# Decoder layer on one core: block-by-block weight products, bias products in column strips, and a first operand copied earlier

## What is computed

```python
q = (x @ wq.T + bq) @ vq.T + cq          # k and v alike
scores = einsum('cbqh,cbkh->cbqk', q, k) / 4      # 32 heads of 16, 4 sequences
o = softmax(scores) @ v;  x = layernorm(x + (o @ wo.T + bo))
conv of kernel size 2 over x (512 -> 2048 channels) + ctx + bias, then LSTM-like gates
x = layernorm(x + [h, c])
x = layernorm(x + dequantised(x) @ (ternary - 1).T + b)
```

## Time and profile before

| | us |
|---|---|
| median of three runs | 2178.78 (2175.0 to 2186.28) |
| profiled execution | 2176.87 |
| its span | 2174.9 |
| TensorE busy | 2090.4 |
| VectorE busy | 1662.9 |
| ScalarE busy | 1313.5 |
| GpSimd busy | 491.3 |

### The profile page before, as it was taken

One profiled execution on the slowest core, in us unless ns is written; L12 is line 12 of the kernel. 1 busy time (PEld: TensorE's weight loads), 2 busy tenths in 40 slices (PEclk: granted clock), 3 DMA queues, 4 the chain that ended last, 5 costly groups with the idle time before them and its releaser, 6 DMA issues. The chain is left out here.

```text
span 2174.9 us, 39902 instructions
## 1 busy us (share of the span) xinstructions
PE 2090.4 (96%) x11304; PEld 1178.6 (54%) x11304; DVE 1662.9 (76%) x1725; ACT 1313.5 (60%) x2429; POOL 491.3 (23%) x972
## 2 busy tenths in 40 slices
PE   8999999999999999999999999999999899988996
PEld 3788775444444444444444444444444477766773
DVE  2333355889899999999989899999998377886786
ACT  0121112778788888888888888888887543443344
POOL 0000000111221221212122122212212372555244
PEclk9999999999999999999999999999999999999997
DMA  4355834564665565564665656656657568744672
GB/s 160 97 155 144 198 107 103 90 131 91 133 134 101 128 140 99 126 135 100 136 128 100 138 114 114 137 94 133 134 101 211 165 229 305 288 174 155 228 265 78
DMA packets 205965, 315.24 MB, mean 145 GB/s; under 512 B 105168, under 2 KB 105168, under 8 KB 193616
## 3 DMA queue, kind: packets, MB, share of 16 engines
q1 hardware_dynamic: 205904, 314.47, 57.5%
HBM read 211.06 MB, written 101.19 MB: 144 GB/s over the span
## 5 line engine op out<-in xcount | busy, mean ns | idle before, releaser
L191 DVE TENSOR_REDUCE neg_max<-psum 128x1 f32<-128x1024 f32 x1024 | 1206.9, 1219 | 137.5 <-PE psum L184 137.4
L558 ACT ACTIVATE probs<-psum 128x512 f32<-128x512 f32 x2048 | 1065.4, 607 | 279.5 <-PE psum L485 277.4
L485 PE MATMUL psum<-q_op,k_op 50*128 50x512 f32 x2048 | 751.7, 450 | 10.6 <-DVE v_op L575 5.2
L485 PEld LDWEIGHTS psum<-q_op,k_op 50*128 50x128 f32 x2048 | 353.8, 192 | 586.7 <-ACT probs L558 567.3
L184 PE MATMUL psum<-k_op,q_op 48*128 48x512 f32 x2048 | 625.2, 482 | 0.0
L494 PE MATMUL psum<-probs,v_op 128*32 128x512 f32 x4096 | 547.2, 606 | 5.8 <-ACT probs L558 2.9
L184 PEld LDWEIGHTS psum<-k_op,q_op 48*128 48x128 f32 x2048 | 390.0, 315 | 23.9 <-issue 8.8
L202 POOL CAST neg_max_parts<-neg_max 128x8 fp32r<-128x8 f32 x128 | 25.2, 197 | 1130.1 <-DVE neg_max L191 1130.1
L149 PE MATMUL psum<-x_wino,conv_w 128*128 128x512 f32 x1152 | 275.2, 395 | 1.1 <-DMA conv_w<-conv_w_parts_dram 1.1
L149 PEld LDWEIGHTS psum<-x_wino,conv_w 128*128 128x128 f32 x1152 | 214.6, 188 | 47.0 <-issue 1.5
L494 PEld LDWEIGHTS psum<-probs,v_op 128*32 128x32 f32 x4096 | 82.5, 108 | 137.0 <-ACT probs L558 78.9
(11 more groups left out here) (99 smaller groups left out, 1692.8 us busy)
## 6 DMA issues: line engine op xcount, KB each, us to landing
q_op<-qk_parts_dram SPq DMA_DIRECT2D x384, 128.0 KB, 4.1
conv_w<-conv_w_parts_dram SPq DMA_DIRECT2D x32, 1536.0 KB, 6.7
qk_parts_dram<-qk_parts SPq DMA_DIRECT2D x128, 256.0 KB, 3.2
k_op<-qk_parts_dram SPq DMA_DIRECT2D x384, 64.0 KB, 4.0
conv_w_parts_dram<-conv_w_parts SPq DMA_DIRECT2D x16, 1536.0 KB, 6.1
attended_dram<-out SPq DMA_DIRECT2D x64, 256.0 KB, 2.2
attended_parts_dram<-o_parts SPq DMA_DIRECT2D x128, 128.0 KB, 2.2
gates<-in_ctx_dram SPq DMA_DIRECT2D x32, 512.0 KB, 7.7
```

What stands on the lines that cost most here:

```text
L191: nc.vector.tensor_reduce(ops["max"][b][:, t:t + 1], mem["pair"][t % 2][:], AX_X, ALU.max, negate=True).then_inc(ops["maxed"], 1)
L485: nc.tensor.matmul(score_bank(i, n, j, last), kop[i][r, j // 2, n // 2 * P:(n // 2 + 1) * P], qop[i][r, j // 2, j % 2 * HALF:(j % 2 + 1) * ...
L558: nc.scalar.activation(probs[n % DEEP][:, j, :], score_bank(k, n, j, last), ACT.Exp, scale=SCALE).then_inc(exp_done, 1)
```

## The change

In `combine`: each piece pair of the query weights has its own semaphore. TensorE goes through the pieces in the outer loop and the four groups in the inner one, so four banks are summed at once. The bias loads are issued after the query weights, ahead of the key weights. The query and key biases come from eight matmuls of 512 moving columns. Their stationary operand is a bias column repeated 32 times, and each of the four (two weights, two halves of the sum) has its own strip of 32 rows of bank 6. VectorE copies bank 6 to `rows`, and four small matmuls with a selecting operand `pick` bring each 128 entries back into columns (and sum the halves). Bias work and the two x splits now stand between the groups. In `project` and `attend`: `v_op` and its fills move to the start of `project` (behind those of `k_op0` and `k_op1`). The first copy of values moves to `project`, as GpSimd's first act there, waiting for the sixteenth value group. TensorE's wait for `ones` at the start of `attend` becomes 4. SP's waits become 5 and 6, which are the same two fills, of `k_op2` and `k_op3`.

```diff
@@ combine, SP @@
+                        done = first_in[c] if s == 0 else w_in[s]
+                        chunk = slice(c * P, (c + 1) * P)
+                        sp.dma_start(wn[s][:, c, :], w_nat[s][chunk, :]).then_inc(done, DMA)
+                        sp.dma_start(vt[s][:, c, :], v_t[s][chunk, :]).then_inc(done, DMA)
+                    if s == 0:
+                        for i in range(2):
+                            sp.dma_start(bc[i][:], b_cols[i]).then_inc(bias_in, DMA)
+                            sp.dma_start(vbc[i][:], vb_cols[i]).then_inc(bias_in, DMA)
+                        sp.dma_start(bvc[:], bv_cols).then_inc(bias_in, DMA)
+                        sp.dma_start(vvb[:], vvb_row.broadcast_to([P, F])).then_inc(bias_in, DMA)
@@ combine, TensorE @@
+                for kc in range(KC):
+                    pe.wait_ge(first_in[kc], 2 * DMA)
                     for mt in range(KC):
-                        if g >= BANKS:
-                            pe.wait_ge(comb_out, g - BANKS + 1)
-                        for kc in range(KC):
...
+                        mm = term(0, mt, kc)
+                        if kc == KC - 1:
+                            mm.then_inc(comb, 1)
+                pe.wait_ge(w_in[1], 2 * KC * DMA)
+                for mt in range(KC):
+                    group(1, mt)
+
+                pe.wait_ge(wide_made, 3)
+                for half in range(2):
+                    for j in range(4):
+                        kc = j % 2 * 2 + half
+                        mm = nc.tensor.matmul(bank[6][VW * j:VW * j + VW, :], b_wide[j // 2][:, kc, :], vt[j // 2][:, kc, :],
+                                              start=(half == 0), stop=(half == 1))
+                mm.then_inc(rows_full, 1)
+                pe.wait_ge(w_in[2], 2 * KC * DMA)
                 for kc in range(KC):
                     mm = nc.tensor.matmul(bank[7], bv_wide[:, kc, :], vt[2][:, kc, :],
                                           start=(kc == 0), stop=(kc == KC - 1))
+                mm.then_inc(v_bias_made, 1)
+                for mt in range(2):
+                    group(2, mt)
+
+                pe.wait_ge(rows_made, 5)
+                for mt in range(KC):
+                    mm = nc.tensor.matmul(bank[6][:, 2 * mt:2 * mt + 2], rows[:, mt * P:(mt + 1) * P], pick[:],
+                                          start=True, stop=True)
                 mm.then_inc(bias_made, 1)
+                for mt in range(2, KC):
+                    group(2, mt)
@@ combine, VectorE, in the loop over the twelve groups @@
+                    if g == 5:
+                        split_x_block(nc, dve, x, 0, 0, DMA)
+                    if g == 2 * KC - 1:
+                        dve.wait_ge(rows_full, 1)
+                        nc.vector.tensor_copy(rows[:], bank[6]).then_inc(rows_made, 1)
+                    if g == 2 * KC:
+                        dve.wait_ge(v_bias_made, 1)
+                        nc.vector.tensor_tensor(v_bias[:], bank[7], vvb[:], ALU.add).then_inc(bias_out, 1)
+                    if g == GROUPS - 3:
+                        split_x_block(nc, dve, x, 1, 1, DMA)
+                        dve.wait_ge(bias_made, 1)
...
@@ project @@
+                for i in range(2):
+                    nc.vector.memset(ops["v"][i][:, :, DH:VW], 1.0).then_inc(ops["ones"], 1)
...
+                pool.wait_ge(v_out, KC + BLK // 2 * KC)
+                copy_values(nc, pool, ops, v_sb, 0, 0)
@@ attend @@
-                sp.wait_ge(ones, 3)
+                sp.wait_ge(ones, 5)
...
-                        sp.wait_ge(ones, 4)
+                        sp.wait_ge(ones, 6)
...
-                pe.wait_ge(ones, 6)
+                pe.wait_ge(ones, 4)
...
-                for i in range(2):
-                    nc.vector.memset(vop[i][:, :, DH:VW], 1.0).then_inc(ones, 1)
...
-                values(0, 0)
```

More of the change, by code:

```diff
@@ L51, in combine @@
         bvc = sb("bv_cols", [P, KC], F32)
+        b_wide = [sb(f"b_wide{s}", [P, KC, VW], F32) for s in range(2)]
         bv_wide = sb("bv_wide", [P, KC, P], F32)
         vvb = sb("vvb", [P, F], F32)
-        w_in = [sem(f"w_in{s}") for s in range(3)]
+        rows = sb("bias_rows", [P, F], F32)
+        pick = sb("pick_rows", [P, 2], F32)
+        first_in = [sem(f"w_in0{c}") for c in range(KC)]
+        w_in = [None, sem("w_in1"), sem("w_in2")]
         bias_in = sem("bias_in")
-        bv_made = sem("bv_made")
+        wide_made = sem("wide_made")
         comb = sem("comb")
@@ L59, in combine @@
         comb_out = sem("comb_out")
+        rows_full = sem("bias_rows_full")
+        rows_made = sem("bias_rows_made")
         bias_made = sem("bias_made")
+        v_bias_made = sem("v_bias_made")
         bias_out = sem("bias_out")
@@ L92, in _ @@
-                pe.wait_ge(bias_in, 6 * DMA)
-                for s in range(2):
-                    for mt in range(KC):
-                        for kc in range(KC):
-                            mm = nc.tensor.matmul(bank[6][:, s * KC + mt:s * KC + mt + 1],
-                                                  vt[s][:, kc, mt * P:(mt + 1) * P], bc[s][:, kc:kc + 1],
-                                                  start=(kc == 0), stop=(kc == KC - 1))
-                mm.then_inc(bias_made, 1)
@@ L100, in _, with term, group @@
-                pe.wait_ge(bv_made, 1)
+                def term(s, mt, kc):
+                    return nc.tensor.matmul(bank[(s * KC + mt) % BANKS], wn[s][:, kc, mt * P:(mt + 1) * P],
+                                            vt[s][:, kc, :], start=(kc == 0), stop=(kc == KC - 1))
+                def group(s, mt):
+                    if s * KC + mt >= BANKS:
+                        pe.wait_ge(comb_out, s * KC + mt - BANKS + 1)
+                    for kc in range(KC):
+                        mm = term(s, mt, kc)
+                    mm.then_inc(comb, 1)
@@ L117, in _ @@
                     nc.vector.tensor_tensor(lo, bank[g % BANKS], hi.bitcast(F32), ALU.subtract).then_inc(comb_out, 1)
[L118 to L124 removed]
+                    if g == 5:
[9 more added lines that the diff above has]
+                        dve.wait_ge(bias_made, 1)
+                        by_s = bank[6][:, 0:2 * KC].rearrange("p (m s) -> p s m", s=2)
+                        for s in range(2):
+                            nc.vector.tensor_tensor(qk_bias[:, s, :], by_s[:, s, :], vbc[s][:], ALU.add).then_inc(bias_out, 1)
 def load_x_block(sp, x, x_t, i, first):
@@ L359, in attend @@
         qop, kop = ops["q"], ops["k"]
-        vop = [sb(f"v_op{i}", [P, 2 * QT, VW], F32) for i in range(2)]
+        vop = ops["v"]
         probs = [sb(f"probs{i}", [P, TILES, HALF], F32) for i in range(DEEP)]
@@ L1444, in build @@
                 "max_in": [[sem(f"max_in{i}{b}") for b in range(2)] for i in range(4)],
+                "v": [sb(f"v_op{i}", [P, 2 * QT, VW], F32) for i in range(2)],
+                "v_ready": sem("v_ready"),
                 "ones": sem("ones"),
```

53 lines of the change are left out of this document (20 added, 33 removed).

## The result

| | us |
|---|---|
| median of five runs of the changed kernel | 2163.71 (2161.57 to 2167.43) |
| median of five runs of the kernel before, beside them | 2178.50 (2175.0 to 2186.28) |
| ratio | 0.9932, 95% interval 0.9908 to 0.9955 |
| profiled execution of the changed kernel, and its span | 2167.43, 2165.4 |

The change takes 14.8 us off. 19.9 were forecast. The profiled execution is the slowest of its five, 3.7 above their median, so its parts are read one by one and not summed against the median.

The account below looks back on a forecast made before the run. TensorE, busy 96% of the span, was taken as the bound. Gains of 17.2 (before the projection), 1.6 (clock) and 1.1 (attention) sum to 19.9 us, forecasting 2158 us, range 2150 to 2168.

Parts of the forecast that it names:

- The forecast's own case: Whole kernel: the summed gain of 19.9 us is kept, giving 2158 us; chance 0.66.
- rival B: Small costs (strips not side by side, clock falls at projection and slot 1) take part of the gain: 2166 us; chance 0.17.
- rival D: Attention: SP late, the wait for maxima recurs at each slot; slower, 2191 us if in 20 slots; chance 0.03.
- rival A: Attention: transfers after the barrier go faster and all gain is kept, 6.1 us more, 2152 us; chance 0.08.
- The start, 6.4 us: Start of combine: first matmuls need only two weight loads, so TensorE starts at 4.2 us, not 10.65.
- Rival C: Start of combine: first weight chunks land with the rest, so 6.4 us go: 2164 us; chance 0.06.
- 48 matmuls in 43.2 us: Combine: the 48 weight matmuls keep the earlier kernel's duration of 43.2 us.
- Bias loads at no cost: Combine: bias loads ahead of the key weights cost nothing; key weights land by about 17.5 us, covered by 2.5 us.
- Bias products 6.7: Combine: strips 2.0, value bias 3.6, selecting products 1.1, together 6.7 us in place of 14.5, gaining 7.8.
- Combine, 17.2 in all: Up to the projection: its first matmul comes at 56.2 us, not 73.37, gaining 17.2 us.
- The clock at the projection, 1.6: Projection's start: after a shorter stand of 2.1 us the clock stays at 2.4 GHz, gaining 1.6 us; lower bound nothing.
- The start of attention, 1.1: Attention, slots 0 and 1: of up to 7.2 us only 1.1 is kept, as row maxima land at 395.6 us.

Follow-up runs that it names:

- e2: Kernel before with the attention edit alone (fills and first copy of v_op moved to project), combine as before: 2183.83 us, ratio 1.0028.
- e8: e2 with SyncE's new store order of e5: 2173.05 us, ratio 0.9976 to the kernel before.
- e9: Kernel before, nothing of the change, with SyncE's new store order of e5: 2174.71 us, ratio 0.9984.
- e4: The changed kernel as it is, timed and traced once more: 2162.96 us, ratio 0.9924 to the kernel before.
- e11: Changed kernel with the second half of the maxima stored earlier in every slot, first slot's order otherwise kept: 2158.31 us, ratio 0.9913.
- e6: Changed kernel plus matmuls with unused results where TensorE would stand at the two barriers: 2162.12 us, ratio 0.9931.
- e7: e5 and e6 together: 2156.74 us, ratio 0.9897 to the kernel before.
- e12: e5 plus unused matmuls ahead of the first weights and the two of e6 ending combine: 2156.36 us, ratio 0.9892.
- e1: Changed kernel with only the combine edits; copy and fills of v_op stay in attend: 2163.21 us, ratio 0.9922.
- e5: Changed kernel; SyncE stores both halves of the maxima together, ahead of other stores (first slot: ahead of taps and operand set 3): 2154.06 us.

## Why the prediction was right or wrong

- **The time.** 2158 was forecast, in 2150 to 2168; 2163.7 came. The direction and the range hold, and the gain is 14.8 where the sum said 19.9. The forecast's own case (its sum kept) did not come; what came lies between it and rival B in size, with rival D's mechanism in it. That the sum came within the range owes something to luck: the terms below were too large by 1.0 for combine and 1.6 for the clock in this trace, and 6.0 for slots 1 to 63 had no term. The 7.2 behind rival A has 4.5 us for a slot 0 at the high clock, which no trace here shows: each has 6.8 us or more at the low one there.
- **The start, 6.4 us:** 4.22 measured for 4.2. Rival C is out. The 10.65 of before was itself a late one: with the same `combine`, the first matmul of e2, e8 and e9 starts at 9.5 to 9.7, so 6.4 us is the top of 5.2 to 6.4.
- **48 matmuls in 43.2 us:** somewhat low. Without the bias products and the first wait they took 44.7 here and 43.4 in e4. The low clock at the start lasted until 10.3 in this trace and until 7.8 in e4's; the projection started at 57.21 and 55.94, and the forecast's 56.2 lies between.
- **Bias loads at no cost:** right, no wait of TensorE before the end of the 48 matmuls. The last key weights landed at 17.6, for 17.5 forecast, and their first group started at 21.1. The five small loads landed 0.2 to 0.3 us apart (9.14 to 10.18).
- **Bias products 6.7:** 1.85 + 3.54 + 0.81 = 6.2. Rival B's strips in 7.2 are out; attention's strips gave the right price.
- **Combine, 17.2 in all:** 16.2 in this trace, 17.4 in e4's; by medians 15.1 with the old order of SyncE, 17.2 and 19.0 with the new one.
- **The clock at the projection, 1.6:** an even chance taken as a gain. The seven traces with this gap unfilled (2.1 to 2.2 us) fell five times and stayed high twice (e4, e11). At 2 in 7 the term is worth 0.5, not 1.6. Its size was right: the first 24 records of the projection took 7.24 us with the fall and 5.69 in e4, 1.55 less. In the three traces where it was filled (e6, e7, e12) the clock never fell there.
- **The start of attention, 1.1:** the mechanism is right for this trace: the landing of the maxima sets slot 1, and TensorE stood 2.6 us (3 forecast). The number is luck in this trace. The 1.1 of the table is read at slot 1's first exponential, ahead of the second stand. At the third score product, where the prediction put it, 26.8 us after the fill were forecast (395.6 - 368.8) and 27.6 measured for 27.8 before: 0.2 kept. In e4 it was 26.7, and 1.1 kept, without a stand. The prediction took the landing for a fixed time, and it is none: in the kernels with the old order in slot 0 the last store was issued 20.6 to 22.2 us after the fill, and landed 26.2 to 29.4 us after it.
- **The step that failed** is the sentence behind it, "So of up to 7.2 us only 1.1 is kept, whatever the clock does in slot 0; TensorE will stand for about 3 us at slot 1's start", in what it leaves out: it prices the stand and nothing behind it. Behind it the clock was low for 10.2 us, and the maxima came late again at slots 5 and 9, with another 10 us of low clock. "If a slot of attention takes longer than before, D is at work" was its own sign, and slots 1, 5 and 9 took longer. Slots 1 to 63 cost 6.0 us more in this trace and 8.4 in e4's. Rival B had 1.1 for the clock at slot 1; the measured term is over five times that.
- **Rival D, 0.03,** was argued away with "SP has room in a slot, once it has caught up". Room was not the point. SyncE has room, but it keeps the second half of the maxima behind a wait for the slot's last product and behind loads that wait for a store. The hand-over alone is D in a smaller form: 5.5 us slower than the kernel before, with 8 waits where D had one at each slot. That the 1.6 us of the earlier trace rows stood in the trace of before once was the warning: one such wait means that the slack there is near zero.

What the traces don't settle: why e1, whose attention is the kernel's of before word for word, had 4.3 us of such waits against 1.6. Both are single executions. With a slack near zero a small difference in the clock or in a landing may decide; this is argued and not shown. The 2.9 us that e9 lies below the kernel before fit the traces: its slots 1 to 63 take 1319.8 us, 3.6 less.

## What to carry over

Before an engine is started earlier, look for whoever feeds it next and is not moved: here the maxima landed no earlier relative to the barrier, and of the 2.8 us won there 0.2 was left at slot 1's third score product in one trace and 1.1 in another. A wait that shows once, with 1 or 2 us, is a resource with no slack, and a gain upstream can turn it into many, some of them with a stretch of low clock behind. In a hand-written queue, a transfer that the critical engine waits for belongs ahead of everything that itself waits; here that reorder of a few lines was worth another 9 us.

## What the runs showed of the hardware that was not expected

- Stands of 1 to 2.5 us at TensorE are often followed by the low clock, and not always: the same 2.1 us gap in the same kernel gave 0.50 in one execution and 1.00 in another. The Trainium skill, page "TensorE: Matmul & The Clock Gate", Part 1, puts the low clock down to how busy the array has been of late; the low stretches of slots 1 and 5, right behind stands of 2.04 and 1.17 us, agree with that in kind, and no run here tells why the same gap goes one way or the other. Halfway through the projection (about 240 us, 257 with the old `combine`) every trace has such a gap: behind 1.8 to 2.0 us the grant stayed at 1.00 in all three traces that had it, and in the eleven with 2.2 to 3.1 us it fell to 0.50.
- The stretch at the low clock can cost more than the stand that leads to it: slot 5 took 3.6 us longer than in e5, and 1.17 of that is the stand, with 7.0 us at 1.2 GHz behind it. In e4's slot 7 it was 4.5 us longer for a stand of 0.96.
- The last of the eight small stores of maxima, issued 20.6 us after the fill in three traces with the same list of SyncE, took 5.6 us to land in e4, 7.0 in the changed kernel and 8.8 in e6.
- How long the first matmuls run at 1.2 GHz varied from 3.1 us (e6, until 7.3) to 6.1 us (the changed kernel, until 10.3) in programs with the same start. Keeping TensorE busy from 1.25 us on brought the high clock at 6.3 us, in one trace.
- A gap of 0.62 us at the barrier did not keep slot 0 at the high clock (e6, e7). Slot 0 has a stand of 1.10 us of its own ahead of e7's fall; that this stand is the cause is not shown.
